# Another order of the fill in a six-layer attention kernel with a linear recurrence

## What is computed

```python
u = gelu(xn @ W_u.T + b_u) * sigmoid(xn @ W_g.T + b_g)   # first gate, second gate
uB = u @ Bm.T
s_t = s_(t-1) @ A.T + uB_t ;  y_t = s_t @ Cm.T + D        # a scan over 256 tokens
for i in range(6):                                        # the stack
    h = attn_layer(shift_tokens(h), ...) + h              # 16 heads, window 32
    h = ffn_layer(shift_tokens(h), ...) + h
out = x + y * silu(h)
```

## Time and profile before

| | us |
|---|---|
| median of 3 runs | 1658.5 (1656.65 to 1660.97) |
| profiled execution, its own time | 1657.53 |
| its span (first to last instruction) | 1655.7 |
| busy PE / DVE / POOL / ACT | 1567.6 / 1416.7 / 1231.0 / 1109.9 |
| start of the first projection (line 500) | 41.58 |
| mean granted TensorE clock | 0.99 |

### The profile page before, as it was taken

One profiled execution on the slowest core, in us unless ns is written; L12 is line 12 of the kernel. 1 busy time (PEld: TensorE's weight loads), 2 busy tenths in 40 slices (PEclk: granted clock), 3 DMA queues, 4 the chain that ended last, 5 costly groups with the idle time before them and its releaser, 6 DMA issues.

```text
span 1655.7 us, 75427 instructions
## 1 busy us (share of the span) xinstructions
PE 1567.6 (95%) x31996; PEld 1312.3 (79%) x31996; DVE 1416.7 (86%) x2757; ACT 1109.9 (67%) x1980; POOL 1231.0 (74%) x1200
## 2 busy tenths in 40 slices
PE   4889999999999999999999999999999999999995
PEld 2468888788888788888888888888888877888884
DVE  4698899889889988988988898989889888888963
ACT  4265777776677777667776766777676776767663
POOL 2377788878778887877887787787778887777851
PEclk9799999999999999999999999999999999999998
DMA  3033223333223323322333322333323333322222
GB/s 112 22 92 73 66 72 81 92 79 86 69 68 73 101 69 89 74 72 68 93 79 82 82 70 69 94 78 82 82 67 73 84 86 82 83 68 66 71 64 81
DMA packets 109742, 127.96 MB, mean 77 GB/s; under 512 B 52064, under 2 KB 55648, under 8 KB 109152
## 3 DMA queue, kind: packets, MB, share of 16 engines
q1 hardware_dynamic: 109408, 123.13, 29.5%
HBM read 20.27 MB, written 2.10 MB: 14 GB/s over the span
## 4 chain that ended last, share of the span: by engine, by line
PE 62%; DVE 12%; ACT 11%; issue 7%; POOL 6%; DMA 1%; SPq 0%; DVEq 0%; POOLq 0%; ACTq 0%
PE F L529 10%; PE O L634 9%; PE VTb L542 7%; PE S L559 6%; PE QKb L500 6%; PE F L599 4%; PE QKb L502 4%; PE QKb L501 4%; DVE t L882 4%; PE S L580 3%; ACT L773 3%; ACT hid L773 2%; DVE mx L910 2%; POOL t L1052 2%; PE S L552 2%
## 5 line engine op out<-in xcount | busy, mean ns | idle before, releaser
L1052 POOL TENSOR_TENSOR t<-t 128x512 f32<-128x512 f32 x384 | 492.2, 1282 | 193.6 <-DVE t L882 180.4
L882 DVE TENSOR_TENSOR t<-QKb,table 128x1024 f32<-128x1024 f32 x384 | 468.3, 1220 | 61.5 <-ACT sq L713 59.4
L1027 POOL TENSOR_TENSOR t<-t,rn 128x512 f32<-128x512 f32 x384 | 401.3, 1045 | 128.5 <-DVE rn L939 128.4
L713 ACT ACTIVATE sq<-QKb 128x512 f32<-128x512 f32 x384 | 231.2, 602 | 238.0 <-PE QKb L502 232.6
L634 PEld LDWEIGHTS O<-PT,V 64*64 64x64 f32 x12288 | 198.6, 134 | 57.5 <-issue 55.3
L634 PE MATMUL O<-PT,V 64*64 64x32 f32 x12288 | 218.4, 220 | 15.9 <-DVE rn L939 15.8
L891 DVE TENSOR_REDUCE ss<-sq 128x16 f32<-128x1024 f32 x192 | 232.0, 1209 | 0.0
L542 PE MATMUL VTb<-cst,t 128*128 128x128 f32 x1536 | 230.5, 272 | 0.1
L529 PEld LDWEIGHTS F<-wo_sb,OT 128*128 128x128 f32 x1536 | 200.5, 191 | 16.3
L1034 POOL TENSOR_TENSOR E<-E,rs 128x512 f32<-128x512 f32 x192 | 200.4, 1044 | 14.6 <-DVE rs L904 14.6
L542 PEld LDWEIGHTS VTb<-cst,t 128*128 128x128 f32 x1536 | 185.4, 141 | 31.1 <-POOL t L1027 2.8
(11 more groups left out here) (152 smaller groups left out, 2769.3 us busy)
## 6 DMA issues: line engine op xcount, KB each, us to landing
V<-v_tok SPq DMA_DIRECT2D x1440, 64.0 KB, 2.0
w_raw<-in_wqkv SPq DMA_DIRECT2D x36, 256.0 KB, 3.0
wo_sb<-in_wo SPq DMA_DIRECT2D x6, 512.0 KB, 4.1
xs<-xm SPq DMA_DIRECT2D x48, 64.0 KB
xs<-xm SPq DMA_DIRECT2D x48, 63.5 KB
w_sb<-in_w SPq DMA_DIRECT2D x6, 341.0 KB
w_sb<-in_w SPq DMA_DIRECT2D x6, 192.0 KB, 3.8
y_spill<-OT SPq DMA_DIRECT2D x1, 1024.0 KB, 4.2
```

What stands on the lines that cost most here:

```text
L713: act.activation(sq[:, v % 4, :], QK_ps, ACT.Square).then_inc(sq_done, 1)
L882: dve.tensor_tensor(t12[:, v:9 + v % 4:8 + v % 4 - v, :].rearrange("p c (h d) -> p c h d", h=8), QK_ps.rearrange("p (h d) -> p h d", h=8). ...
L1027: pool.tensor_tensor(w, w, rn[:, vv // 4, 8 * (vv % 4):8 * (vv % 4 + 1)].unsqueeze(2) .to_broadcast([P, 8, DH]), ALU.mult).then_inc(qk_nor ...
L1052: pool.tensor_tensor(w, w, t12[:, 8 + v % 4, :].rearrange("p (h c d) -> p h c d", h=8, c=2)[:, :, ::-1, :], ALU.add).then_inc(add_done, 1)
```

## The change

On PE, the four first-gate products come first (line 467 with k = 0), and then the four second-gate products, each of the first three with its squaring behind it; the wait for the third power now stands only ahead of the last second-gate product. On ACT, `stage` comes right behind the four Gelus, and the rounding of weight blocks 2 and 3 moves behind the Sigmoids, in one loop with blocks 4 and 5; the square root waits for two DVE settings in place of four. On DVE, the two bf16 copies and their wait for `cst` move from ahead of the statistics to behind the normalisation, and `stage_low` moves from the end of the fill to between the third kept power and the gates' products. The waits on counts follow the new order. No instruction that computes or moves data is added or removed.

```diff
--- before.py
+++ after.py
@@ -461,11 +461,13 @@
 
             for c in range(4):
                 pe.wait_ge(xT_done, c + 1)
+                pe.matmul(banks[c][:, :], rw[:, 0, :], xf[:, 512 * c:512 * (c + 1)],
+                          start=True, stop=True).then_inc(rec_mm, 1)
+            for c in range(4):
                 if c == 3:
                     pe.wait_ge(pow_done, 3)
-                for k in range(2):
-                    pe.matmul(banks[4 * k + c][:, :], rw[:, k, :], xf[:, 512 * c:512 * (c + 1)],
-                              start=True, stop=True).then_inc(rec_mm, 1)
+                pe.matmul(banks[4 + c][:, :], rw[:, 1, :], xf[:, 512 * c:512 * (c + 1)],
+                          start=True, stop=True).then_inc(rec_mm, 1)
                 if c < 3:
                     square(c + 1, banks[7])
 
@@ -673,9 +675,14 @@
                 col = W_COLS[c]
                 act.copy(w_hi[:, col:col + 512], w_raw[:, c % 2, :]).then_inc(hi_done[c], 1)
 
+            def stage(src, par):
+
+                act.copy(x_hi[0:64, par, :], src[0:64, :]).then_inc(x_staged, 1)
+                act.copy(x_hi[64:P, par, 1:N], src[64:P, 0:N - 1]).then_inc(x_staged, 1)
+
             for c in range(2):
                 round_weights(0, c)
-            act.wait_ge(set_dve, 4)
+            act.wait_ge(set_dve, 2)
             act.wait_ge(mv_done, TILES)
             act.activation(rst[:, :], mv[:, :, 1], ACT.Sqrt, bias=eps[:, 0:1]).then_inc(sd_done, 1)
             for c in range(4):
@@ -683,26 +690,18 @@
                 act.copy(xf[:, 512 * c:512 * (c + 1)], banks[c][:, :]).then_inc(xT_done, 1)
             act.wait_ge(in_rec, 32)
             for c in range(4):
-                act.wait_ge(rec_mm, 2 * c + 1)
+                act.wait_ge(rec_mm, c + 1)
                 act.activation(U[:, 512 * c:512 * (c + 1)], banks[c][:, :], ACT.Gelu,
                                bias=rb[:, 0:1]).then_inc(rec_act, 1)
-            for c in range(2, 4):
-                round_weights(0, c)
+            act.wait_ge(set_pool, 6)
+            stage(xf[:, 0:N], 0)
             for c in range(4):
-                act.wait_ge(rec_mm, 2 * c + 2)
+                act.wait_ge(rec_mm, 4 + c + 1)
                 act.activation(G[:, 512 * c:512 * (c + 1)], banks[4 + c][:, :], ACT.Sigmoid,
                                bias=rb[:, 1:2]).then_inc(rec_act, 1)
 
-            def stage(src, par):
-
-                act.copy(x_hi[0:64, par, :], src[0:64, :]).then_inc(x_staged, 1)
-                act.copy(x_hi[64:P, par, 1:N], src[64:P, 0:N - 1]).then_inc(x_staged, 1)
-
-            act.wait_ge(xT_done, 4)
-            act.wait_ge(set_pool, 6)
-            for c in range(4, 6):
+            for c in range(2, 6):
                 round_weights(0, c)
-            stage(xf[:, 0:N], 0)
 
             def step(s, par, b_):
                 for v in range(SLOTS):
@@ -784,9 +783,6 @@
         def _(dve):
             dve.memset(eps[:, :], 1e-5).then_inc(set_dve, 1)
             dve.memset(minus_half[:, :], -0.5).then_inc(set_dve, 1)
-            dve.wait_ge(in_cst, 16)
-            dve.tensor_copy(ident_bf[:, :], ident).then_inc(set_dve, 1)
-            dve.tensor_copy(mask_bf[:, :], cst[:, C_MASK:C_MASK + 4 * KEYS]).then_inc(set_dve, 1)
 
             dve.wait_ge(in_x, 16)
             for t in range(TILES):
@@ -802,6 +798,10 @@
                 dve.tensor_scalar(x_all[:, t, :], x_tok[:, t, :], mv[:, t, 0:1], rst[:, t:t + 1],
                                   ALU.subtract, ALU.mult).then_inc(ln_done, 1)
 
+            dve.wait_ge(in_cst, 16)
+            dve.tensor_copy(ident_bf[:, :], ident).then_inc(set_dve, 1)
+            dve.tensor_copy(mask_bf[:, :], cst[:, C_MASK:C_MASK + 4 * KEYS]).then_inc(set_dve, 1)
+
             def keep_power(r, bank_):
 
                 dve.wait_ge(pow_ready, r)
@@ -810,6 +810,17 @@
 
             for r in range(1, 4):
                 keep_power(r, banks[7])
+
+            def stage_low(src, par, done):
+
+                wait(dve, x_staged, done + 2)
+                dve.tensor_tensor(x_lo[0:64, par, :], src[0:64, :], x_hi[0:64, par, :].bitcast(F32),
+                                  ALU.subtract).then_inc(x_low, 1)
+                dve.tensor_tensor(x_lo[64:P, par, 1:N], src[64:P, 0:N - 1], x_hi[64:P, par, 1:N].bitcast(F32),
+                                  ALU.subtract).then_inc(x_low, 1)
+
+            dve.wait_ge(set_pool, 6)
+            stage_low(xf[:, 0:N], 0, 0)
 
             for c in range(4):
                 dve.wait_ge(rec_act, 4 + c + 1)
@@ -833,17 +844,6 @@
                     dve.wait_ge(scan_ready, i + 1)
                     dve.tensor_scalar(yT.rearrange("p b n -> p (b n)")[:, 512 * c:512 * (c + 1)], banks[3 + c % 2][:, :],
                                       rb[:, 2:3], None, ALU.add).then_inc(yT_done, 1)
-
-            def stage_low(src, par, done):
-
-                wait(dve, x_staged, done + 2)
-                dve.tensor_tensor(x_lo[0:64, par, :], src[0:64, :], x_hi[0:64, par, :].bitcast(F32),
-                                  ALU.subtract).then_inc(x_low, 1)
-                dve.tensor_tensor(x_lo[64:P, par, 1:N], src[64:P, 0:N - 1], x_hi[64:P, par, 1:N].bitcast(F32),
-                                  ALU.subtract).then_inc(x_low, 1)
-
-            dve.wait_ge(set_pool, 6)
-            stage_low(xf[:, 0:N], 0, 0)
 
             def step(s, par, b_):
                 if b_ == 0:
```

## The result

Median before 1658.5 us (7 runs, 1656.65 to 1661.29), after 1652.7 us (7 runs, 1651.59 to 1658.21); ratio 0.9972, 95% interval 0.9961 to 0.9982. The forecast was 1652.1. The ratio alone puts the gain at 4.6 us, between 3.0 and 6.5, so whether it exceeds 0.3% was left open by these runs. The executions with a profile are single ones: 1657.53 before, 1658.21 after. Their ends say nothing of the change; stretch by stage they say a good deal.

A forecast was written before the change was run, and what follows sets the result against it. The prediction took the fill's chain across DVE, ACT and PE, 41.58 us ahead of the first projection, as what the change affects; 1.28 + 5.14 = 6.4 us off the median 1658.5 gave 1652.1, range 1647.0 to 1657.5.

The forecast's parts named there:

- The front, 1.28 us: Start of the fill: without DVE's casts and constants wait, the square root's table load comes 1.28 us earlier, as cap.
- PE's order and the Gelus: Fill, PE and ACT: Gelus run together, `stage` done at 25.34, first Sigmoid at 26.65, in the times of before.
- DVE is late next, not ACT: Gates' products: DVE's third kept power and `stage_low` bind; 3.3 us gained where ACT alone would give 4.6.
- The products' end, 31.16: DVE's four gate products, spaced 0.60, end at 31.16 in the times of before, against 34.45.
- uB stage at full clock: End of fill: PE idles only 0.4 us, so uB is priced at full clock; slow would mean 1.5 us less gain.
- Weight blocks hidden: Fill's roundings: block 5 done by 36.4, ACT's first square due 37.4; cost 0, margin 1.0 us.
- 5.14 + 1.28 = 6.4: Whole fill: 5.14 us from the reordered gates and uB stage plus 1.28 from the front give 6.4 us.
- The rest only shifts: Everything behind the fill keeps its old spacing and only moves earlier by the 6.4 us.
- the first rival: Behind the fill, PE's second half-clock stretch disappears or is much shorter: 10.6 us gained, 1647.9; chance 0.15.

The follow-up runs named there:

- the front alone: Kernel before with only DVE's casts and their wait for the constants moved behind the normalisation: ratio 0.9994, medians 1657.52 and 1659.43.
- the old pairs: Changed kernel with PE's old order, the two gates' products in pairs: ratio 0.9977, first projection at 38.70.
- the second execution: Changed kernel unaltered, run and profiled again beside the last experiment: profile 1650.50 us, median 1651.13, ratio 0.9954 to the kernel before.
- POOL held: Changed kernel with POOL's rests of blocks 2 to 5 waiting for DVE's four gate products: ratio 0.997 to the kernel before.
- fillers: Changed kernel, blocks 2 and 3 rounded ahead of `stage`, four unused PE products in each of slots 1 to 10: ratio 0.9959; with tail products too, 0.997.

## Why the prediction came out right, point by point

- **The front, 1.28 us.** Right. Statistics at 7.24, load at 12.11 behind the rounding. By the timeline it is 1.35 there and, for the front alone, 1.2 at the first projection; by the runs alone it is not shown (0.9994). The cap of 1.28 was none: the rounding of block 1 does move, since its transfer lands at another time in each execution, and the load came 1.35, 1.75 and 1.99 earlier (12.11, 11.71, 11.47).
- **PE's order and the Gelus.** Right. All Gelus in one run, `stage` done by 24.57, and with the old pairs the inner fill is 2.4 longer (2.0 without the loss at half clock). The Sigmoids' table load again took 1.30 to the first Sigmoid (24.59 to 25.89), as in the row that the sum went by.
- **"DVE is late next, not ACT".** Right as to the order: the third kept power (27.02), then `stage_low`, then the products from 27.83, though 0.45 later than the 27.38 of the sum. The stalled second-gate product ended late with it, at 28.20 and not near 27.7. The 0.45 is the first gate product, which I costed at 0.86 from the earlier trace rows, a row at full clock. With the earlier front it began at 18.55, ahead of the change to full clock at 19.55, and cost 0.50 more; where the clock was full in time (the second execution) the products began 15.22 behind the square root's load, 15.20 by the sum.
- **The products' end, 31.16 - 1.28 = 29.88.** Wrong: it was 31.40. The step that failed is the spacing of 0.60 for the fourth product. In the weight blocks' part I moved POOL's rest of block 2 to 31.5 less a duration of 1.24, so beside those very products, and asked only who waits for it, not what it does to DVE. The fill of the trace before did not show it, since that rest ran there from 29.47 to 31.95 and the products from 31.95: end to end, by luck. The Trainium skill (SBUF — State Buffer, "Who interferes with whom") states the exclusion: a VectorE instruction with two inputs in SBUF contends with a GpSimd instruction that reads SBUF, and the one that was issued first holds the ports. The traces agree: 1762 and 1758 ns with the overlap in the two executions of the changed kernel, 680 to 693 in all products without it. But the same trace shows it further on, which I missed. The rotary tables, made anew at each layer, take 0.41 us where POOL is idle and up to 2.06 beside its products (minimum, median, maximum in ns):

```profile
L854 DVE TENSOR_TENSOR table<-cst,scales x12: 411/1102/2060, 41.4 to 1324.8; 128x256 f32<-128x256 f32 x12
```

- **uB stage at full clock; first projection 0.4 us behind its last kept power.** Right: uB at 28.58, granted clock 1.00.
- **Weight blocks hidden.** Right, with block 5 rounded from 35.23 to 35.85, and the first square at 37.58.
- **5.14 + 1.28 = 6.4.** The fill gave 5.0 and 6.1 in the two profiled executions. The 1.07 of the exclusion and the 0.50 or nothing of half clock at the first products are the difference, and the second profile also had a front 0.7 earlier than I reckoned, which made up for most of it. With POOL held, which takes the exclusion alone away, the inner fill is 5.0 shorter than before, 5.2 without the loss at half clock, where the sum had 5.14.
- **The rest only shifts.** Nearly. The lead at slot 16 is 5.5 and 6.6 us, at the last slot (383) 3.8 and 7.1. In between it moves in jumps of 0.1 to 1.5 us at single slots, up and down, not by drift. The slow stretch was 17 us long and not 20, which the sum did not hold, and gave 0.5 us at slot 2. It did not vanish in any kernel without fillers, so the first rival is out as put; its price was mis-sized, as the fillers showed. That the half clock differs between executions of one kernel is seen in the tail (0.53 granted from 1613 to 1624 in one execution of the changed kernel, 1.00 in the other) and at the start (full from 19.55 in one, from 17.89 in the other), as the Trainium skill (TensorE: Matmul & The Clock Gate, "The HAM clock gate") says of the gate's raster, which does not start with the kernel.
- **The size.** The median moved by 5.8 us and in the second session, by the ratio, by 0.46%, 7.6 us; the first session's ratio says 4.6. The forecast of 6.4 lies between. The two ratios are 3 us apart, and their intervals, 0.9961 to 0.9982 and 0.9941 to 0.9968, only just overlap. "Faster by over 0.3%" is borne out by the second and left open by the first. That the median came within 0.6 us of the forecast is in part luck, as far as the profiles tell: the exclusion that the sum lacked (1.07) was made up, in the second profile, by things that it did not hold either, a front 0.7 earlier and the shorter half-clock stretch (0.5).

No experiment can be told by its ratio to be faster than the changed kernel. What stays open: why the transfer of instructions that PE waits for near 885 us comes late in some profiles, and what sets the place of the tail's slow stretch.

## What to carry to other kernels

When a step is moved in time, list what will now run beside it, on the other engines too. A DVE instruction with two inputs in SBUF costs nearly the whole remaining length of a POOL instruction that it meets (1.07 us here, of 1.21 that were left). Where the two happened to be end to end in the trace of before, look for another pair of the same kind in it: here the rotary tables, up to five times as long beside POOL as alone. In a long pipelined kernel judge a change of the fill by the time of its first steady instruction and by the same slot in both traces; the end of a single profiled execution carries 4 us of clock and 1.5 us of stall that have nothing to do with it. And ask at which clock PE starts: in one execution the first gates' products, 1.25 us earlier than before, fell ahead of the change to full clock, and 0.5 us of the gain went back.

## What was not expected of the hardware

The exclusion works both ways: POOL's next rest, which came while DVE's product was in, took 1.72 us instead of 1.27, and the rotary tables took 1.38 to 2.55 instead of 0.76 beside POOL's rests. Extra products that kept PE at full clock through the recurrence's slots bought 1.3 to 1.8 us there in one profile, which they cost again in the denser slots behind, and nothing in another, in which a piece at half clock was left. And PE's instructions can come late in a long kernel: 1.0 to 1.9 us of idle time in the midst of a run of small products, ending 2.2 to 2.5 us after a transfer of the instruction queue starts.
